# First attention of a four-layer block: the row maxima ride in spare rows of the stacked queries, the picking rows in spare rows of the keys

## What is computed

```python
def _L0_xattn_ref(x, context, Wq, bq, Wk, bk, Wv, bv, Wo, bo):
    q = x @ Wq.T + bq;  k = context @ Wk.T + bk;  v = context @ Wv.T + bv
    # 16 heads of 16
    scores = jnp.einsum('bhtd,bhcd->bhtc', q, k) / jnp.sqrt(16)
    attn = jax.nn.softmax(scores, axis=-1)
    out = jnp.einsum('bhtc,bhcd->bhtd', attn, v)
    return out.reshape(B, T, D) @ Wo.T + bo
x = x + jnp.tanh(g_xattn[0]) * _L0_xattn_ref(_layernorm(x), ctx_1024, ...)
```

## Time and profile before

| | |
|---|---|
| median of 3 executions | 1048.76 us (1048.45 to 1050.56) |
| the profiled execution | 1049.8 us span; its own time is not given apart from that |
| setup | 0 to 44.8 us |
| slots -1 to 15 | 44.8 to about 287 us |
| PE busy | 922.7 us (88%), 6641 products |
| DVE, ACT, POOL busy | 770.3, 598.5, 327.3 us |
| L1033, score products | 256, 70.5 us busy |
| L1036, subtracting products | 256, 66.1 us busy |

### The profile page before, as it was taken

How to read it: one execution, slowest core, us unless ns; L and a number is a source line. 1 busy time by engine, 2 the same in 40 slices (tenths; PEclk the granted TensorE clock), 3 DMA queues, 4 the chain that set the end, 5 groups by cost and what they waited for, 6 DMA issues and landing times. The chain is left out here.

```text
span 1049.8 us, 20050 instructions
## 1 busy us (share of the span) xinstructions
PE 922.7 (88%) x6641; PEld 818.1 (78%) x6641; DVE 770.3 (73%) x1551; ACT 598.5 (57%) x1041; POOL 327.3 (31%) x500
## 2 busy tenths in 40 slices
PE   4899999998969999960279969999999989999998
PEld 4778877777758887750279868999999978988898
DVE  6537888887656988998987746777777858666771
ACT  5257767766656757889858635666556533222230
POOL 5312323330119914437724321222222222112200
PEclk8999999999988999995589979999999979999999
DMA  6557745585073307879401367555555310010001
GB/s 202 164 136 222 203 128 137 150 266 129 2 277 157 160 41 225 272 254 391 181 41 43 110 134 174 125 123 125 124 122 122 76 41 1 21 41 21 20 20 41
DMA packets 100138, 137.01 MB, mean 131 GB/s; under 512 B 42711, under 2 KB 75735, under 8 KB 97383
## 3 DMA queue, kind: packets, MB, share of 16 engines
q1 hardware_dynamic: 99446, 134.00, 44.5%
q10 hardware_dynamic: 320, 1.05, 0.5%
q0 software_dynamic: 304, 1.10, 0.3%
HBM read 68.47 MB, written 45.82 MB: 109 GB/s over the span
## 5 line engine op out<-in xcount | busy, mean ns | idle before, releaser
L2817 ACT ACTIVATE f_h<-bank,f_b 128x512 f32<-128x512 f32 x64 | 43.4, 690 | 112.9 <-PE bank L44 65.1
L923 DVE TENSOR_REDUCE a_maxima<-bank 128x4 f32<-128x308 f32 x128 | 60.3, 471 | 43.6 <-PE bank L1011 42.6
L842 ACT ACTIVATE a_prob<-bank 77x512 f32<-77x512 f32 x128 | 72.4, 588 | 21.1 <-PE bank L1036 20.8
L42 PE MATMUL bank<-f_xt_hi,f_w_all 128*128 128x512 f32 x192 | 78.2, 407 | 5.9 <-DMA f_xt_lo<-x_spill 3.9
L43 PE MATMUL bank<-f_xt_lo,f_w_all 128*128 128x512 f32 x192 | 76.6, 399 | 0.0
L44 PE MATMUL bank<-f_xt_hi,f_w_all 128*128 128x512 f32 x192 | 76.6, 399 | 0.0
L44 PE MATMUL bank<-f_w_hi,f_h_lo 128*128 128x256 f32 x256 | 72.4, 283 | 0.0
L43 PE MATMUL bank<-f_w_lo,f_h_hi 128*128 128x256 f32 x256 | 72.3, 282 | 0.0
L42 PE MATMUL bank<-f_w_hi,f_h_hi 128*128 128x256 f32 x256 | 72.0, 281 | 0.0
L1033 PE MATMUL bank<-a_stack,a_kb 96*77 96x256 f32 x256 | 70.5, 300 | 0.5 <-ACT a_mt L835 0.5
L1687 PE MATMUL bank<-a_values,a_prob 77*128 (+1 forms) x512 | 67.3, 275 | 0.0
(11 more groups left out here) (336 smaller groups left out, 3209.4 us busy)
## 6 DMA issues: line engine op xcount, KB each, us to landing
u_spill<-f_ubuf SPq DMA_DIRECT2D x48, 256.0 KB, 2.5
f_w_all<-u_spill SPq DMA_DIRECT2D x24, 512.0 KB, 5.8
a_stack<-a_queries SPq DMA_DIRECT2D x16, 512.0 KB, 5.2
a_q_max<-a_q_hi SPq DMA_DIRECT2D x30, 256.0 KB, 4.5
a_kb<-a_key_spill SPq DMA_DIRECT2D x96, 77.0 KB, 2.6
xres<-in_x SPq DMA_DIRECT2D x16, 256.0 KB, 5.2
a_queries<-a_q_hi SPq DMA_DIRECT2D x16, 256.0 KB, 3.9
a_queries<-a_q_lo SPq DMA_DIRECT2D x16, 256.0 KB, 4.8
```

Of the source, the lines that this page charges most:

```text
L42: nc.tensor.matmul(out, w_hi, m_hi, start=start, stop=False)
L842: act.activation(prob[0:S, n % 4, :, :].rearrange("p a b -> p (a b)"), (S0, S1)[n % 2][0:S, :], ACT.Exp, scale=SCALE).then_inc(probs, 1)
L923: dve.tensor_reduce(maxima[:, t, 4 * k:4 * k + 4], MX[:, 0:4 * SE].rearrange("p (h s) -> p h s", s=SE)[:, :, 0:S], AX.X, ALU.max).then_inc ...
L2817: act.activation(h[:, n % 2, :], hbank[n % 4][:, :], ACT.Gelu, bias=b1[:, n:n + 1]).then_inc(h_ready, 1)
```

## The change

The subtracting products go. The tiles `pick` and `mt` go with them. Rows 96 to 111 of `stack`, unused so far, take the maxima, copied by ScalarE once for each of the eight pairs: four pairs in the step `mt` at its old place, four in a new step `mu` of the next slot, between the exponentials of `s0` and `s1`. The source is the same 16x256 of `MX`, read four times by one instruction. Rows 96 to 111 of `kb` take the picking rows, written once at the end of the setup by two ScalarE copies of 16x1248 that stand for the one copy of 16x1248 earlier in the setup; their input comes by two DMAs instead of one. The score product takes 112 rows instead of 96. Two memsets on POOL go.

The waits: `s0` needs the copy `mt`, `s2` and the next `mx0` need the copy `mu`. Before, `mx0` needed the copy `mt`.

```diff
-        pick = sb("pick", [P, HEADS, SE], F32R)
-        mt = sb("mt", [P, 2, T], F32R)
...
-                sp.dma_start(pick_raw[:], picks).then_inc(small_in, 16)
+                for a in range(2):
+                    sp.dma_start(pick_raw[ROWS:ALL_ROWS, a, :, :],
+                                 picks.rearrange("r (p a) s -> r a p s", a=2)[:, a, :, :]).then_inc(small_in, 16)
...
-                act.wait_ge(cleared, 1)
-                act.activation(pick[0:HEADS, :, :], pick_raw[:], ACT.Copy).then_inc(picked, 1)
...
+                for n in range(2):
+                    act.activation(kb[ROWS:ALL_ROWS, n, :, :, :].rearrange("r a p s -> r (a p s)"),
+                                   pick_raw[ROWS:ALL_ROWS, :, :, :].rearrange("r a p s -> r (a p s)"),
+                                   ACT.Copy).then_inc(picked, 1)
                 act.activation(warm[:], gate_raw[:], ACT.Exp)
...
-        ACT_SLOT = "s0 s1 xt turn0 s2 st2 s3 p1 s4 turn1 s5 p3 s6 at0 q1 turn2 s7 xn rk p5 mt p7".split()
+        ACT_SLOT = "s0 mu s1 xt turn0 s2 st2 s3 p1 s4 turn1 s5 p3 s6 at0 q1 turn2 s7 xn rk p5 mt p7".split()
...
-                elif what == "mt":
-                    act.wait_ge(mt_ready, b + 1)
-                    act.activation(mt[0:HEADS, par, :], MX[0:HEADS, 0:T], ACT.Copy).then_inc(mt_copied, 1)
+                elif what in ("mt", "mu"):
+                    if what == "mt":
+                        act.wait_ge(mt_ready, b + 1)
+                    pairs = slice(0, PAIRS // 2) if what == "mt" else slice(PAIRS // 2, PAIRS)
+                    act.activation(stack[ROWS:ALL_ROWS, par, pairs, :],
+                                   MX[0:HEADS, 0:T].unsqueeze(1).to_broadcast([HEADS, PAIRS // 2, T]),
+                                   ACT.Copy).then_inc(mt_copied, 1)
...
-                            pe.wait_ge(mt_copied, b)
+                            pe.wait_ge(mt_copied, b * 2)
...
-                        pe.wait_ge(mt_copied, b + 1)
+                        pe.wait_ge(mt_copied, b * 2 + 1)
                         if isinstance(b, int) and b == 0:
-                            pe.wait_ge(picked, 1)
-                            pe.wait_ge(cleared, 3)
+                            pe.wait_ge(picked, 2)
+                    elif n == 2:
+                        pe.wait_ge(mt_copied, b * 2 + 2)
...
-                        pe.matmul(out, kb[0:ROWS, par, a, pair, 0:S], stack[0:ROWS, par, pair, :],
-                                  start=True, stop=False)
-
-                        last = pe.matmul(out, pick[:, 2 * pair + a, 0:S], mt[:, par, :], start=False, stop=True)
+                        last = pe.matmul(out, kb[0:ALL_ROWS, par, a, pair, 0:S], stack[0:ALL_ROWS, par, pair, :],
+                                         start=True, stop=True)
```

More of the change, by code:

```diff
@@ L96, in stacked_attention @@
     ROWS = 96
+    ALL_ROWS = ROWS + HEADS
     SE = S + S % 2
@@ L317, in move_queries @@
                     sp.wait_ge(kb_stored, 32)
-                    sp.wait_ge(cleared, 3)
+                    sp.wait_ge(cleared, 1)
                 if not (isinstance(b, int) and b < 2):
@@ L412, in stacked_attention @@
             gate_raw = tmp("gate_raw", [P, 1])
-            pick_raw = tmp("pick_raw", [HEADS, HEADS, SE])
+            pick_raw = tmp("pick_raw", [P, 2, PAIRS, SE])
             w_in, c_in = [sem(f"w_in{n}") for n in range(3)], [sem(f"c_in{n}") for n in range(3)]
@@ L431, in stacked_attention @@
                     for part, kv, w in (("hi", kv_hi, w_hi), ("lo", kv_lo, w_lo))}
-            N_SMALL = 6
+            N_SMALL = 7
             block = setup.enter_context(nc.Block())
@@ L474, in _ @@
                     pool.memset(keys[:, :, :, S:SE].bitcast(F32), 0.0).then_inc(k_cleared, 1)
-                pool.memset(pick[:].bitcast(F32), 0.0).then_inc(cleared, 1)
-                pool.memset(kb[:].bitcast(F32), 0.0).then_inc(cleared, 1)
-                pool.memset(mt[:].bitcast(F32), 0.0).then_inc(cleared, 1)
+                pool.memset(kb[0:ROWS].bitcast(F32), 0.0).then_inc(cleared, 1)
                 ln_inverse(pool, 0)
@@ L658, in stacked_attention @@
         PE_FIRST = "s0 s1 xt u10 mx0 u11 s2 s3 mx1 u12 s4 q0 u13 mx2 p1 s5 mx3 u14 p3 s6 mx4 u15 s7 mx5 u16 t0 q1 u17 mx6 p5 t1 mx7 u18 u19 mt t2 p7".split()
-        ACT_FIRST = "s0 s1 xt s2 e5 s3 p1 s4 e6 s5 p3 e7 s6 q1 e8 s7 xn p5 e9 mt p7".split()
+        ACT_FIRST = "s0 mu s1 xt s2 e5 s3 p1 s4 e6 s5 p3 e7 s6 q1 e8 s7 xn p5 e9 mt p7".split()
         PE_LAST = "key0 t3 key1 key2 at0 key3 key4 pr0 pr1 key5 key6 key7 key8 key9 key10 key11".split()
@@ L972, in step @@
                         pe.wait_ge(c_kept, 32)
-                        pe.wait_ge(mt_copied, B)
+                        pe.wait_ge(mt_copied, 2 * B)
                     elif n == 1:
```

## The result

The changed kernel takes a median of 1075.24 us (1067.06 to 1078.24), 1.0236 times the kernel before, with an interval of 1.0206 to 1.0266: slower by 26 us where 2 us less were forecast. The profiled execution is the least of these, 1067.06 us, with a span of 1065.3 us against 1049.8. The other three ran at a mean granted clock of 0.913 to 0.922 against its 0.924; where they lost their further 6 to 11 us no profile tells.

The account below looks back on a forecast made before the run. It took a loop over the keys' DMA, with VectorE dense behind mx0, to bound the slots, not TensorE. Terms 0.8 + 2.1 - 2.9 - 0.4 - 1.1 - 0.3 - 0.4 = -2.2 gave 1046.6 us, range 1041.0 to 1051.0.

Parts of the forecast that it names:

- The clock: Rival: slots of the first attention drop to clock 0.87, some 5 us of each costing 0.7 more; 1056 us, chance 0.03.
- The front: Copy start to mx0: 3.17 us against 3.10 in slots 3 to 14, +0.8 us; slots 1 and 2, +2.1 us.
- The backs: mx0 to the next copy: -2.9 us in slots 3 to 14, -0.4 more in 13 and 14, -1.1 in 1 and 2.
- the terms for these slots: Slots 1 to 14: fronts +0.8 and +2.1 us, backs -2.9, -0.4 and -1.1 us.
- The copies: ScalarE's copies of the maxima, 16x1024 instead of 16x256: 1.02 us each, bounds 0.37 and 1.23.
- a cheap and a dear copy: Rivals on ScalarE's copy: towards 0.37 us gives 1038 us, chance 0.06; 1.23 us gives 1052.5 us, chance 0.08.
- The wait for the keys: mx0's DMA wait, 0.80 us in each of 12 slots, goes; a ScalarE wait of about the same size replaces it.
- Slot 0: Longer copy +0.65 us against 12 removed products: between +0.6 and -1.0, taken as -0.3 us.
- the setup: Ahead of the slots: its two final copies and one more DMA cost 0, with -1 to +0.5 us as bounds.
- The back does not shrink: Rival: xs or the second maxima come as late as now, losing the backs' gain; 1050.2 us, chance 0.18.
- PE is the bound: Rival: TensorE bounds the first attention's slots, so the whole 30.7 us go; 1018.1 us, chance 0.03.

Follow-up runs that it names:

- e9: The changed kernel with 16 more score products in every slot, none ahead of the first maxima product: 1072.85 us, 1.0241 of the kernel before.
- e3: The changed kernel with 8 unused products put ahead of the first maxima product of slots 1 to 14, into TensorE's wait: 1050.43 us, 1.0045.
- e5: The changed kernel itself, unaltered, measured again: 1069.38 us, 1.0204 of the kernel before.
- e6: The changed kernel with the 8 score products of s4 to s7 run twice, in the back of each slot: 1073.21 us, 1.0194 of the kernel before.
- e2: The kernel before without its 256 subtracting products, so the maxima are not subtracted, and without the new copies: 1040.47 us, 0.9939.
- e7: The changed kernel with ScalarE's second copy right behind the first in the slots, and behind the first query tile in the lead-in: 1047.12 us, 0.9981.
- e14: e7 with 4 unused products ahead of mx4 of slots 10 to 14 and 4 ahead of mx0 of slots 11 and 12: 1044.23 us, 0.9962.
- e12: e7 with xt ahead of ScalarE's first two exponentials, and TensorE's xt ahead of s0 and mx1 ahead of s3: 1052.70 us, 1.0049.
- e10: e7 with unused products in its last slots, 6 ahead of the weights' transposes, 4 each ahead of mx0 and mx4: 1046.21 us, 0.9987.

## Why the prediction was wrong

**The step that failed is the rival "The clock"**: chance 0.03, price 0.7 us a slot, because "the idle pieces stay near 1 us". The pieces came out about as forecast, 1.13 to 1.40 us ahead of `mx0`. What failed is the conclusion that pieces of this length leave the clock up. In the kernel before they did, four times, up to 1.66 us; with 16 products fewer in a slot and such a piece in every slot they brought it down in half of the slots, and e9 shows that it can happen with those products back.

The price was too low as well. I let only the 5 us that PE stands in the chain be slowed, at a mean clock of 0.87, and no row shows these 5 us. A fall really runs at the lower level for some three and a half microseconds or some ten, and in it PE is busy throughout (10.20 of 10.20 us in slot 3), so that all of it is stretched: by 3.6 to 3.8 us in each of slots 3, 7 and 11, 0.8 to 1.2 in slots 1, 5 and 9, and 2.5 by the two falls of slot 14. And I took the level from a stretch with less of PE's time busy and not from what PE does ahead of a fall. The size of it: e3 has the change's fronts and keeps the clock up through slot 14. Its backs sum to 150.3 us, those of the change to 166.7. The clock costs 16.4 of the profiled 17.7 us, 1.2 a slot. Why one slot falls and the next, with the same wait, does not stays open.

**The front was mis-sized**, 3.45 for 3.17 us. Slot 3, from the timeline of ACT:

```profile
105.14 1.01 ACT L838 ACTIVATE a_stack<-bank 16x1024 fp32r<-16x1024 f32 x1 [0.45 <-PE bank L1023]
106.18 0.38 ACT L855 ACTIVATE a_heads_out<-bank 128x256 f32<-128x256 f32 x1
106.71 0.59 ACT L847 ACTIVATE a_prob<-bank 77x512 f32<-77x512 f32 x1
107.33 1.01 ACT L838 ACTIVATE a_stack<-bank 16x1024 fp32r<-16x1024 f32 x1
```

`s0` follows the first copy as worked out (106.21), and the exponential too. But `mu` starts 0.62 behind the exponential, not 0.49: two exponentials overlap, an exponential and this copy did not. And `mx0` starts at 108.59, 0.25 behind the end of `mu`, not 0.05, though `s0` does take 0.06. Why either is so stays open. Fronts of slots 1 to 14 so cost +6.9 us (e3 against before) where +2.9 was forecast.

**The backs were nearly right**: with the clock up they are 10.75 to 10.84 in slots 3 to 11 of e3 (forecast: 0.24 less than 11.02, so 10.78), 10.40 in slots 1 and 2, and 0.5 less than before in slots 13 and 14. Together -5.7 where -4.4 was forecast. So at an undisturbed clock the terms for these slots would have read +6.9 - 5.7 = +1.2, not -1.5: the change as written would be at best the same, and e3's 1.0045, which has its fillers' small cost and a disturbed slot 0 and 15 in it, goes with that.

**The other steps.** The copies: 1.012 us for 1.02, so the rivals of a cheap and a dear copy fall; the Trainium skill's price ("ScalarE: Activation LUTs", "What ACT_TABLE_LOAD costs"), 1.04, was 0.03 high. The wait for the keys went, as forecast. Slot 0 took 0.2 us more, inside its bounds. The first copy of slot 0 starts 0.4 us earlier, inside the bounds of the setup; but with the same setup it starts at 53.3 us in e5 and at 56.6 in e6, so a single execution says little of that term. "The back does not shrink" falls. "PE is the bound" falls: without products and without copies e2 gains 0.6%, where PE's busy share would have promised 30.7 us. I read the Trainium skill ("Perfetto Trace Analysis", "Identifying the Most-Contended Engine") too simply there: the section says itself that the busy share of matmuls is no good measure for TensorE, and asks for that of the weight loads. In slot 6 these are busy for 10.95 of 14.00 us, less than DVE's 11.90.

What misled was the step from PE not being the bound to its idle time being free.

## What to carry to other kernels

TensorE's idle time was not free here where it came as one piece. Before work is taken off it or a wait is added, list the longest waits that it will have in each turn of the loop, beside those it has now; where one grows, move the work that it waits for (e7), or place something into the wait (e3, e14), ahead of counting products. And read the granted clock by stretch ahead of the busy share, since a slowed engine looks busier.

## What the runs showed of the hardware

- The granted clock fell to the lower level behind single waits of 0.7 to 1.7 us on TensorE (0.74 in e7, 1.24 in slot 3 of the change, 1.49 in e2), and at three shorter ones close together (0.41, 0.61 and 0.26 in e12), in one slot and not in the next with the same wait. It stayed up behind four waits of 1.03 to 1.66 us in the kernel before, and behind one of 1.20 in e7. A fall lasted some three and a half microseconds (five of eight in the change, all five in e9) or some ten (three in the change).
- Which slot falls differs from one execution to another: seven of fourteen in each of the two profiles of the change, slot 14 alone in both. The times of the change spread by 11 us and those of e10 by 3; those of the kernel before spread by 8 to 10 beside the experiments, so it is not shown that the falls are what spreads them.
- The Trainium skill, "TensorE: Matmul & The Clock Gate", section "A second HAM failure mode: psum-queue depth-cycling", tells of a kernel whose frequent short idle pieces make the clock swing between its levels. The change, with a piece of 1.13 to 1.40 us in every slot and eight falls in fourteen slots, agrees.
- A ScalarE copy that reads 256 columns four times (16x1024 out) takes 1.012 us, one that reads them once 0.373: what is written sets its time, not the source.
- GpSimd's addition of 16x1024 (1.91 us) makes a VectorE operation beside it 2.6 times as long (0.56 to 1.43 us).
